# Inverse roots of the head norms: GpSimd's power replaced by a bit-pattern guess and three Newton steps on VectorE, with three kinds of steps placed later

## The reference, cut to what matters

```python
def layernorm(x, g, b):
    mu = jnp.mean(x, axis=-1, keepdims=True)
    var = jnp.mean(jnp.square(x - mu), axis=-1, keepdims=True)
    return (x - mu) * jax.lax.rsqrt(var + EPS) * g + b
...
q = layernorm(q, ln_g, ln_b)
k = layernorm(k, ln_g, ln_b)
...
P = jnp.einsum('bsd,dr->bsr', x, U1)
H = jax.nn.gelu(jnp.einsum('bsr,rf->bsf', P, V1) + b1)
Q = jnp.einsum('bsf,fr->bsr', H, U2)
```

## Time and profile before

| what | value |
|---|---|
| median of three runs | 7277.4 us |
| the profiled execution | 7297.03 us |
| its span, first to last instruction | 7295.2 us |
| mean granted TensorE clock | 0.952 |
| busy: PE, DVE, ACT, POOL | 6573.1, 3609.2, 3207.4, 2959.5 us |
| start of iteration 0, of iteration 1, of iteration 15 | 258.17, 513.38 and 4657.80 us |
| length of an iteration with head and tail | 293 to 305 us |

### The profile page before, as it was taken

One profiled execution on the slowest core, in us unless ns is written; L12 is line 12 of the kernel. 1 busy time (PEld: TensorE's weight loads), 2 busy tenths in 40 slices (PEclk: granted clock), 3 DMA queues, 4 the chain that ended last, 5 costly groups with the idle time before them and its releaser, 6 DMA issues. The chain is left out here.

```text
span 7295.2 us, 92018 instructions
## 1 busy us (share of the span) xinstructions
PE 6573.1 (90%) x35805; PEld 3225.4 (44%) x35869; DVE 3609.2 (49%) x7012; ACT 3207.4 (44%) x5697; POOL 2959.5 (41%) x1969
## 2 busy tenths in 40 slices
PE   3789999999989999999999999985899999999999
PEld 1223333333333333333333333222788888766666
DVE  2555555655656556566565565641766666200000
ACT  1355555555555555555555555551322222111111
POOL 5327447365483663844736538223222222100000
PEclk8799999999999999999999999995999999999999
DMA  2341332432323323133242231302344444411111
GB/s 60 67 77 49 65 56 63 72 60 51 63 59 68 67 52 76 44 70 60 60 74 59 55 71 47 57 16 79 104 153 159 156 164 158 156 52 52 52 52 41
DMA packets 364931, 546.03 MB, mean 75 GB/s; under 512 B 59824, under 2 KB 281984, under 8 KB 364240
## 3 DMA queue, kind: packets, MB, share of 16 engines
q1 hardware_dynamic: 321232, 498.18, 28.2%
q10 hardware_dynamic: 43264, 41.95, 1.7%
HBM read 387.94 MB, written 151.28 MB: 74 GB/s over the span
## 5 line engine op out<-in xcount | busy, mean ns | idle before, releaser
L1148 DVE TENSOR_REDUCE mx<-psum 128x1 f32<-128x401 f32 x4096 | 2193.4, 570 | 1722.6 <-PE psum L744 1711.7
L999 ACT ACTIVATE probs<-psum 128x512 f32<-128x512 f32 (+1 forms) x3328 | 1920.1, 597 | 1149.4 <-PE psum L766 1145.8
L744 PE MATMUL psum<-kst,qst 96*128 96x401 bf16 x4096 | 1434.7, 352 | 268.3 <-DVE mx L1148 202.7
L766 PE MATMUL psum<-qst,kst 99*128 99x512 bf16 (+1 forms) x3328 | 1299.7, 394 | 152.1 <-ACT probs L999 116.6
L744 PEld LDWEIGHTS psum<-kst,qst 96*128 96x128 bf16 x4096 | 404.2, 99 | 1553.3 <-DVE mx L1148 1246.0
L777 PE MATMUL psum<-probs,vaug 128*17 128x512 f32 x6656 | 904.5, 616 | 0.0
L598 POOL TENSOR_TENSOR ssq<-ssq,powers 128x64 f32<-128x64 f32 (+1 forms) x80 | 722.2, 9027 | 6.7
L766 PEld LDWEIGHTS psum<-qst,kst 99*128 99x128 bf16 (+1 forms) x3328 | 330.9, 100 | 860.8 <-ACT probs L999 463.0
L1415 POOL TENSOR_TENSOR disp<-disp,rz 128x2048 f32<-128x2048 f32 x64 | 294.9, 4608 | 909.2 <-DVE rz L1634 909.2
L1434 PE MATMUL psum<-phi,xT 128*128 128x128 f32 x4096 | 511.7, 279 | 39.8 <-DMA xT<-xnT_scratch 32.5
L1434 PEld LDWEIGHTS psum<-phi,xT 128*128 128x128 f32 x4096 | 479.9, 193 | 87.4 <-issue 79.8
(11 more groups left out here) (185 smaller groups left out, 7761.3 us busy)
## 6 DMA issues: line engine op xcount, KB each, us to landing
xnb<-xn_scratch SPq DMA_DIRECT2D x256, 512.0 KB, 3.7
kst<-k_planes SPq DMA_DIRECT2D x384, 200.1 KB, 9.1
k_planes<-pl SPq DMA_DIRECT2D x96, 384.0 KB, 3.2
y_scratch<-ysb ACTq DMA_DIRECT2D x128, 256.0 KB, 3.4
disp<-y_scratch SPq DMA_DIRECT2D x16, 2048.0 KB, 9.4
vaug<-v_scratch SPq DMA_DIRECT2D x64, 442.0 KB, 3.4
v_scratch<-vst SPq DMA_DIRECT2D x48, 544.0 KB, 3.1
cin<-in_ctx SPq DMA_DIRECT2D x48, 512.0 KB, 3.8
```

The source lines that it names most:

```text
L744: mm(to[:, 0:PW], qst[g][0:NP, j, t * P:(t + 1) * P], kst[g][0:NP, j, k0:k0 + PW], start=True, stop=True).then_inc(m_full, 1)
L766: mm(bank[S_BANK[n % 2]][0:m, :], kst[g][0:NR, j, c * P:c * P + m], qst[g][0:NR, j, :], start=True, stop=True).then_inc(s_full, 1)
L999: fn(probs[0:m, 4 * (k % 2) + j, :], bank[S_BANK[j % 2]][0:m, :], ACT.Exp, scale=float(HD) ** 0.5).then_inc(s_exp, 1)
L1148: v.tensor_reduce(mx[:, u // 4, u % 4:u % 4 + 1], bank[M_BANK[r % 2]][:, 0:PW], AX.X, ALU.max).then_inc(m_free, 1)
```

## The change

POOL no longer adds the constant or takes the power in `kn`; it only multiplies. DVE does both in `ssq`, as a chain of twelve linked instructions behind the sum: plus 16 EPS, a shift of the bit pattern, its subtraction from a constant (a first guess of the inverse root), and three Newton steps of three instructions each. POOL is told of it when the last one is done. `ssq` and `kn` stand 0.6 of a step later, and `gtanh` and `gpost` of the first four tiles, `gpre` of the third and fourth, the fifth `V1` and the first `U2` up to two thirds of a step later. Nothing else moves.

```diff
@@ woven
     for n, done in ((0, ("K", 3)), (1, ("Q", 1)), (2, ("K", 7)), (3, ("K", 11)), (4, ("K", 12))):
         put(head[done] + 0.01, 1, "sq", n)
-        put(head[done] + 0.7, 1, "ssq", n)
-        put(head[done] + 0.72, 1, "kn", n)
+        put(head[done] + 1.3, 1, "ssq", n)
+        put(head[done] + 1.32, 1, "kn", n)
...
-        put((10.67, 11.0, 11.34, 11.67, 15.67, 16.67, 17.67, 18.67)[f], -1, "V1", f)
-        put((11.01, 11.5, 12.34, 13.0, 16.34, 17.34, 18.34, 19.34)[f], -1, "gpre", f)
-        put((12.0, 12.67, 13.67, 14.34, 18.0, 19.0, 20.0, 21.0)[f], -1, "gtanh", f)
-        put((12.01, 12.68, 13.68, 14.35, 18.01, 19.01, 20.01, 21.01)[f], -1, "gpost", f)
-        put((15.34, 16.34, 17.34, 18.34, 20.0, 21.0, 22.0, 23.0)[f], -1, "U2", f)
+        put((10.67, 11.0, 11.34, 11.67, 15.9, 16.67, 17.67, 18.67)[f], -1, "V1", f)
+        put((11.01, 11.5, 12.67, 13.67, 16.34, 17.34, 18.34, 19.34)[f], -1, "gpre", f)
+        put((12.34, 13.34, 14.0, 14.67, 18.0, 19.0, 20.0, 21.0)[f], -1, "gtanh", f)
+        put((12.35, 13.35, 14.01, 14.68, 18.01, 19.01, 20.01, 21.01)[f], -1, "gpost", f)
+        put((15.67, 16.34, 17.34, 18.34, 20.0, 21.0, 22.0, 23.0)[f], -1, "U2", f)
@@ scaled (POOL)
-                r = ssq[:, n % 2, 0:m, :]
-                link(pool.tensor_scalar(r, r, HD * EPS, None, ALU.add))
-                link(pool.tensor_tensor(r, r, powers[:, 0:1, None].broadcast_to((P, m, H)), ALU.pow))
+                r = rstd[:, n % 2, 0:m, :]
@@ square_sums (DVE)
-                v.tensor_reduce(ssq[:, n % 2, 0:m, :], sq[:, 0:m, :].rearrange("p c (h d) -> p c h d", h=H), AX.X,
-                                ALU.add).then_inc(ssq_done, 1)
+                z, y, t = ssq[:, 0:m, :], rstd[:, n % 2, 0:m, :], root[:, 0:m, :]
+                link(v.tensor_reduce(z, sq[:, 0:m, :].rearrange("p c (h d) -> p c h d", h=H), AX.X, ALU.add))
+                link(v.tensor_scalar(z, z, HD * EPS, None, ALU.add))
+                link(v.tensor_scalar(t.bitcast(I32), z.bitcast(I32), 1, None, ALU.logical_shift_right))
+                link(v.tensor_scalar(y.bitcast(I32), t.bitcast(I32), -1, ROOT_SEED, ALU.mult, ALU.add))
+                for i in range(3):
+                    link(v.scalar_tensor_tensor(out=t, in0=y, scalar=-0.5, in1=z, op0=ALU.mult, op1=ALU.mult))
+                    link(v.tensor_tensor(t, t, y, ALU.mult))
+                    ins = v.scalar_tensor_tensor(out=y, in0=t, scalar=1.5, in1=y, op0=ALU.add, op1=ALU.mult)
+                    if i < 2:
+                        link(ins)
+                ins.then_inc(ssq_done, 1)
```

More of the change, by code:

```diff
@@ L30 @@
 EPS = 1e-5
+ROOT_SEED = 0x5F3759DF
 NB = 5
@@ L314, in stage_one @@
         sq = sb("sq", [P, 4, D])
-        ssq = sb("ssq", [P, 2, 4, H])
+        ssq = sb("ssq", [P, 4, H])
+        rstd = sb("rstd", [P, 2, 4, H])
+        root = sb("root", [P, 4, H])
         bst0 = sb("bst0", [P, QT, 6])
```

## The result

The changed kernel takes **7316.7 us** (median of 9 runs, 7303.78 to 7343.27) where the kernel before, run beside it on the same chip, takes 7290.5 (9 runs, 7277.04 to 7309.19): a ratio of **1.0037**, 95% interval 1.002 to 1.0054. It is slower by 0.4%, inside the forecast's likeliest case. The profiled execution took 7307.78 us, its span 7306.0; before 7297.03 and 7295.2.

The account below looks back on a forecast made before the run. PE bounds the kernel (90% busy), its gaps ending a chain from POOL's late power through DVE or ACT. Terms: -17.0 + 20.1 = +3.1 us an iteration, +43 for 14, iteration 0 +10, prologue -17: +36, giving 7313 us; range 7195 to 7385.

Parts of the forecast that it names:

- the forecast's likeliest case: Whole kernel: slower than before by over 0.3%, chance 0.52.
- A hold on DVE: DVE gone from the pieces for sum and chain: 4.3 us; beside POOL 6.3 for the queries, 7 for block 4.
- Gelu: Steps 12-15 and 19-22: POOL has four powers less to do, the tanh waits vanish; -6.5 us an iteration.
- Steps 9 and 10: Step 9's old idle and clock loss goes, -5.5 us; queries' hold stalls PE 4.5, clock 2.0, +6.5 an iteration.
- Step 16: Block 2's sum and chain, POOL idle: PE stall 2.8 us, clock 1.2, together +4.0 us an iteration.
- Step 27: Old idle and clock loss goes, -5.0 us; block 4's hold of 7 stalls PE 5.5, clock 2, +7.5 an iteration.
- Prologue: Before the iterations, nothing beside POOL: a chain is almost 8 us shorter than the power's way; -17 us.
- Iteration 0: First iteration: has the new holds and no gelu to win; +10 us.
- The rival that the chain runs free: Steps 9 and 27: POOL does not lengthen the chain, holds 4.3 and 2.8 us; total 7190 us, chance 0.22.
- that of short instructions: Every hold 1.2 us shorter, so stalls of steps 5, 9, 16 and 27 fall; total 7246 us, chance 0.06.
- The rival of one overlap: Steps 9 and 27: POOL lengthens only one chain, or its power was less on the path; about 7260 us, chance 0.15.
- The rival of the clock: Stalls over 4 us, longer than any now (3.3 at most), bring a longer clock drop; 7380 to 7418 us, chance 0.12.

Follow-up runs that it names:

- Run 4: Changed kernel with POOL's scaling of the queries moved ahead of the planes of block 0; 0.9979 of the kernel before, 7292 us.
- run 1: Changed kernel with the chain kept on DVE but every step at its old place; 0.9941 of the kernel before, 7274 us.
- run 3: Changed kernel with one Newton step in place of three, so less exact inverse roots; 0.9747 of the kernel before.
- run 5: Changed kernel with POOL's bias addition (`base`) moved behind the scaling of block 4; 0.9999 of the kernel before, 7315 us.
- Run 10: Changed kernel with queries' and block 4's chains cut in three, a step apart; blocks 2, 3 and gelu at old places; 0.971 of the kernel before, 7114 us.
- run 6: Changed kernel with blocks 2, 3, 4 at old places and queries' scaling ahead of block 0's planes; 0.9925 of the kernel before, 7258 us.
- run 11: Run 10 with two Newton steps instead of three; 0.9659 of the kernel before.
- run 9: Changed kernel with each chain cut in three parts a whole step apart, block 3's at once; 0.9843 of the kernel before.
- run 8: Changed kernel with each chain cut in three parts a third of a step apart; 1.0127 of the kernel before, 7412 us.

## Why the prediction was right

The sign came out, and the mechanism with the largest terms. That the time is right to 4 us (7313 forecast, 7317 measured) is luck: the forecast added 36 us to 7277.4, the median of three runs, and the median of nine is 7290.5, so the change really added 26 us. Even that is as near as it is because errors of both signs take each other off.

- **A hold on DVE.** Forecast 4.3 us for blocks 0, 2, 3; measured 4.23. For the queries 6.3, measured 5.72, so POOL adds 1.5 us and not 2.0. Run 4 shows that this is POOL's doing: with the planes moved the hold fell to 4.23.
- **Gelu.** -6.5 forecast; 12-14 went from 19.1 to 16.7 and 18-22 from 34.8 to 29.9, -7.3, and step 15 rose by 0.5: -6.8. Shown by run 1 to be POOL's relief, and not the new places: it has the same 16.7 and 29.9 with the old ones.
- **Steps 9 and 10.** -5.5 for the old wait and +6.5 for the hold, +1.0; measured 16.87 to 17.52 us, +0.65. The stall is 3.49 us (iteration 8, across steps 9 and 10), not 4.5; the clock took more than its 2.0 (5.6 us at half clock in step 10; PE was busy 2.7 us longer than in run 3 with the same work). The two errors nearly cancel, which is luck.
- **Step 5.** +2.1; measured +1.65 over steps 5 to 7.
- **Step 16.** +4.0; measured +5.3 over 16 and 17. The stall was nearly right (2.8 forecast, 2.48 measured). The clock's term of 1.2 was too small: with 5.9 us at half clock in steps 16 and 17, what is left of the 5.3 us for it is 2.8.
- **Step 25.** 0; steps 24 to 26 did not move.
- **Step 27.** -5.0 and +7.5, +2.5; measured +1.1 over 27 to 29. The step that failed here is "busy until about 3660.4, longer by 4": the four `xn` hardly hold DVE, `base` does. The hold was 5.78 us and not 7. Alone, in the prologue, it takes 2.93; of the 2.85 us more, run 5 took 2.07 away by moving `base`. The stall was 4.51 and not 5.5.
- **Prologue** -17, measured -15.8. **Iteration 0** +10, measured -0.2: the term was mis-sized because the kernel before had stalls of its own there, which the forecast left out. Its steps 12, 13 and 27 took 12.2, 8.7 and 12.1 us; they take 4.7, 6.7 and 5.8 now. The new holds cost 15.6 us there (steps 5, 6, 9, 10, 16 and 17) and these three steps give back 15.9.

The three terms that were too high (step 27, iteration 0, the stall of step 9) and the ones too low (clock in 16, what comes after iteration 14) cancel only in part: +11 us between the profiled executions where +36 was forecast, +26 between the medians. The rival that the chain runs free is refuted by the hold of 5.72 us and by run 4; that of short instructions by 0.225 us for each of the nine with two tensors and 0.195 for the other three. The rival of one overlap was half right: the queries' came whole, block 4's by its one addition. The rival of the clock has the wrong rule. It expected more where a stall is longest, but the clock went furthest over its forecast behind the shortest of the three: 2.8 us for 1.2 at the stall of 2.48, 2.7 for 2.0 at that of 3.49, and 2.1 for 2.0 at that of 4.51 (iteration 8, steps 27-29: PE's busy time is 16.71 us, in run 3 14.60). The 3.3 us that it called the longest stall of the kernel before was the longest for DVE alone: the earlier trace rows has one of 3.5 for ACT.

The wider reading: the changed kernel gives back at four places what it wins. One of them, block 2 in step 16 with +5.3 us, exists only because of the new place, and block 4's is 2.3 us longer for it (27-29: 19.6 us with the old place, 21.9 with the new one). At the other two, block 0 and the queries, the new place is the better one, by 2.3 and 2.5 us (run 1). Run 10 keeps 12.2 us an iteration (296.0 to 283.9) of the 17.0 that the forecast had as gain; no run with three Newton steps kept more.

## What to carry to other kernels

Work moved to an engine that feeds the bottleneck is priced by where it lands, not by its length: the same 4.2 us cost nothing in step 15, 1.7 us in step 5 and 5.3 in step 16. Read for each place how far ahead the bottleneck may run and what it does meanwhile, keep the pieces short with several of the reductions that the bottleneck waits for in between, and keep them away from POOL's additions, subtractions and casts of large tensors. And try each half of a change alone: here the chain was worth 0.6%, part of it in the prologue, and the new table cost it 1% between the ratios, or 2.9 us an iteration (0.6%) by the steps other than 38 to 40.

## What had not been expected of the hardware

- **The clock doubles the price of a stall, or leaves it alone.** PE waits in step 38 for the row maxima, which arrive by DMA. There an idle time of 1.74 us or less left step 39 at 5.57 us (before: iterations 1, 3, 5, 6, 8 to 14), and one of 2.2 to 3.6 us made it 10.0 to 10.8 (before: iterations 2, 4, 7; changed: 4, 10, 11). The line between the two is not sharp: in other runs idle times of 2.2 to 2.9 us in step 38 left step 39 at 5.57 (run 1, iterations 4, 6 and 7; run 6, iteration 7). In step 16 an idle time of 2.76 us came with 5.9 us at half clock, one of 1.20 with none (run 3). The step-38 case comes and goes from iteration to iteration in every kernel, 7 to 12 us each time in steps 38 to 40, three times in the kernel before and ten times in run 11. It may be much of the scatter between executions, which one trace of each kernel can't show; what makes that DMA late was not tried.
- **Not all POOL work holds DVE alike.** The Trainium skill (SBUF — State Buffer, the section on who interferes with whom) says that a VectorE instruction with two SBUF inputs and a GpSimd instruction that reads SBUF exclude each other, the second one fully blocked. The trace agrees for POOL's tensor-by-tensor additions (0.17 us becomes 2.22), and not for its normalisation by two scalars per row, during which most of DVE's 0.17 us instructions of two inputs ran in 0.17 and the longest took 0.50. Nor does it agree for POOL's power of two tensors: in run 9 the one in `lna` (128x4, 1.04 us) has 24 two-input instructions of DVE's 128x64 Newton steps wholly inside it, and they ran in 0.21 to 0.23. The same section has TENSOR_REDUCE never contending on trn2: the trace agrees, as in run 8 the 14 sums of block 2 that began while a 1.27 us multiplication of POOL was under way took 1.21 us each, as elsewhere.
